# One prologue rebuilt: batch 0 ahead, distances in half blocks between projections, context products in the last pair

## The chip, the core and the metric

The kernel runs on one core of one Trainium2 chip. The time is device microseconds of a whole execution. Below it stand the five engines: TensorE (PE, with its weight loads PEld), VectorE (DVE), ScalarE (ACT), GpSimd (POOL), and the queue SP, which issues the DMAs. Each works through its own instructions in order and waits on semaphores.

## What is computed

One decoder layer over x (2, 1024, 256), in float32: a distance attention with 16 heads of width 64, a cross attention over a context of 77 rows, and a mixture of 8 experts. What the change touches is the first, and the keys and values of the second:

```python
P = X @ W_in + b_in                    # X = layernorm(x); Q, K, V, G for 16 heads
W = (EPS + sqrt(max(q2 + k2 - 2 Q K^T, 0))) ** -2
W = W / (EPS + sum(W))                 # over the keys
H = G * (W @ V)
x = x + H @ W_out + b_out
k, v = ctx @ Wk.T + bk, ctx @ Wv.T + bv        # cross attention, 77 rows for each batch
```

## The kernel before, in words

The work of the first attention is cut into 16 pairs of heads: pairs 0 to 7 are the 16 heads of batch 0, pairs 8 to 15 those of batch 1 (`PAIRS`, `QP` = 8). Each pair has T = 1024 tokens as 8 key blocks of 128 (`SB`), the two heads side by side. HALF is 512 tokens. All products are made from high and low parts (`_hi`, `_lo`), so a projection is 12 matmuls of 128x512 (`STEPS`), and a block of distances 16 (four terms, two heads, two halves).

What is done for a pair, by engine:
- TensorE: `project_qk` (Q, then K, through the bank `ps_p`), `norm_q` and `norm_k` (squared norms), `project_g`, `project_v`, `turn_v`, then for each block `distances` (L510, into `ps_s`) and, one pair later, `values` (L522) and `row_sums` (L535).
- VectorE: copies out of the banks with the bias (`copy_q` L852, `copy_k` L858, `copy_g` L891, `copy_vt` L886, `copy_v` L895), high and low parts (`split_high`, `split_low`, L864 to L870), `norm_rows` (L874, L876), `copy_k2` (L881), and for each block the two `guard` operations (L927, max with 0, one for each head) which free the banks for the next block.
- ScalarE: roots (L1364), then after a table load logarithm (L1370) and exponential (L1372) over chunks of blocks.
- GpSimd: splits weights (L1488, L1492), squares Q and K (L1505, L1511), and adds up half of the row sums.

In the pair loop, pair p's values, pair p+1's distances and pair p+2's Q and K projections are interleaved. Before it stands a prologue, and the change is in it. It runs: SP issues all of x, the constants, biases, context, cross-attention weights, and then the first projection weights. VectorE takes the statistics of all 16 row tiles, ScalarE the square root (L1341), VectorE normalises 16 tiles (L827). Meanwhile TensorE makes the context products (L410, L414), which VectorE later turns into `k_blk` and `v_x` (`context`). TensorE turns the rows of both batches (L425, 8 groups of 4), ScalarE and VectorE write their high (L1346) and low (L833) parts. Then Q, K of pair 0, the norms, Q, K of pair 1, G and V of pair 0, and after these the eight blocks of distances of pair 0, each of which waits until both guards of the block before are done (`max_ok`). There is no planner; the order on each engine is that of the written code.

Of the kernel before, what the change touches and what calls it, by code (L numbers as in the profile page):

```python
# [5 lines left out]
ALU = mybir.AluOpType  # L6
# [7 lines left out]
P = 128  # L14
# [78 lines left out]
def program(nc, x, ctx_t, mask, w_in, b_in, w_out, w_x, b_cols, rows_in, gate_w, w1, w2, w3, consts, r_consts, out):  # L93
    with ExitStack() as ctx:
# [114 lines left out]
        x_first = wts[:, 1, 0:4, :].rearrange("p a (b d) -> p (a b) d", d=D)  # L209
# [40 lines left out]
        names = ("x_in", "c_in", "stats_ok", "aggr_ok", "std_ok", "rstd_ok", "xn_ok", "tr_ok", "xnt_ok",  # L250
# [17 lines left out]
        C_IN = 16 * (1 + 8 + DC + 4 + 1 + 4 + 1 + 1)  # L268
        xn = wts[:, 0, 0:4, :].rearrange("p a (b d) -> p (a b) d", d=D)
# [4 lines left out]
        def _(sp):  # L274
            sp.dma_start(x_first, x.rearrange("b (n p) d -> p (b n) d", p=P)).then_inc(S_.x_in, 16)
            sp.dma_start(cst[:], consts).then_inc(S_.c_in, 16)
            for k in range(4):
                for h in range(2):
                    src = b_in[k // 2, (k % 2) * DH:(k % 2 + 1) * DH]
                    sp.dma_start(b_all[h * DH:(h + 1) * DH, k], src).then_inc(S_.c_in, 16)  # L280
            for c in range(DC):
                sp.dma_start(ctx_sb[:, c], ctx_t[c * P:(c + 1) * P]).then_inc(S_.c_in, 16)
            for k in range(4):
                sp.dma_start(w_x_sb[:, k], w_x[k].rearrange("(c p) n -> p c n", p=P)).then_inc(S_.c_in, 16)
            sp.dma_start(b_qk_x[:], b_cols).then_inc(S_.c_in, 16)
            for k in range(4):
                sp.dma_start(brow[:, k], rows_in[k:k + 1].partition_broadcast(P)).then_inc(S_.c_in, 16)
            sp.dma_start(mask_i[:], mask.partition_broadcast(P)).then_inc(S_.c_in, 16)
            sp.dma_start(gate_sb[:], gate_w.rearrange("(c p) e -> p c e", p=P)).then_inc(S_.c_in, 16)
# [21 lines left out]
            load_qk(0, 0)  # L311
            load_vg(0, 0)

# [3 lines left out]
            load_qk(1, 1)  # L317
            load_qk(2, 2)
# [86 lines left out]
        def _(pe):  # L405
            pe.wait_ge(S_.c_in, C_IN)
            for b in range(B):
                for c in range(DC):
                    for cc in range(DC):
                        pe.matmul(ps_o[:, (b * DC + c) * KC:(b * DC + c + 1) * KC], w_x_sb[:, 1, cc, c * P:(c + 1) * P],  # L410
                                  ctx_sb[:, cc, b * KC:(b + 1) * KC], start=cc == 0, stop=cc == DC - 1)
            for b in range(B):
                for cc in range(DC):
                    mm = pe.matmul(ps_o[0:KC, HALF + b * D:HALF + (b + 1) * D], ctx_sb[:, cc, b * KC:(b + 1) * KC],  # L414
                                   w_x_sb[:, 2, cc, :], start=cc == 0, stop=cc == DC - 1)
            mm.then_inc(S_.kv_mm, 1)
            pe.wait_ge(S_.xn_ok, 1)
            for n in range(NT // 4):
                for c in range(DC):
                    k = n * DC + c  # L420
                    if k >= 4:
                        pe.wait_ge(S_.xnt_ok, k - 3)
                    dst = ps_s[:, (k % 4) // 2, (k % 2) * 512:(k % 2) * 512 + 512]
                    for i in range(4):
                        mm = pe.transpose(dst[:, i * P:(i + 1) * P], xn[:, 4 * n + i, c * P:(c + 1) * P], ident)  # L425
                    mm.then_inc(S_.tr_ok, 1)
            pe.wait_ge(S_.xnt_ok, NT // 4 * DC)
# [11 lines left out]
            def project_qk(p, i0, i1, rows_before):  # L439
                for i in range(i0, i1):  # L440
                    if i == 0:
                        pe.wait_ge(S_.wqk_ok, 2 * p + 2)
                        if rows_before is not None:
                            pe.wait_ge(S_.rln_ok, rows_before)
# [7 lines left out]

            def norm_q(n):
# [8 lines left out]
            def norm_k(n):  # L462
                pe.wait_ge(S_.sqk_ok, n + 1)
                pe.wait_ge(S_.qn_ok, n + 1)
                for b in range(SB):
                    mm = pe.matmul(ps_s[:, 0, 2 * b:2 * b + 2], k_sq[:, b * P:(b + 1) * P], cst[:, C_SK:C_SK + 2], start=True, stop=True)
                mm.then_inc(S_.k2_mm, 1)

            def project_v(n, keys):
                pe.wait_ge(S_.wvg_ok, 2 * n + 2)  # L470
                pe.wait_ge(S_.k_cp, keys)
# [4 lines left out]
            def project_g(n):  # L476
                if not (isinstance(n, int) and n == 0):
                    pe.wait_ge(S_.max_ok, NB * n + NB)
                for i in range(STEPS):
                    mm = project_step(ps_s[:, 1], wvg_hi, wvg_lo, n, 1, i)  # L480
                mm.then_inc(S_.g_proj, 1)

            def turn_v(n):
                pe.wait_ge(S_.vt_ok, n + 1)
                pe.wait_ge(S_.kv_ok, 1)
                if not (isinstance(n, int) and n == 0):
# [5 lines left out]
            def distances(n, b):  # L492
                if b == 0:
# [4 lines left out]
                    done = 1 if isinstance(n, int) and n == 0 else n  # L498
                    pe.wait_ge(S_.vt_ok, done)
                    pe.wait_ge(S_.g_ok, done)  # L500
                else:
# [1170 lines left out]
```

## Time and profile before

| | us |
|---|---|
| median of 3 runs (lowest, highest) | 1659.29 (1654.48, 1662.12) |
| the profiled execution | 1656.51 |
| its span, first to last instruction | 1654.3 |
| mean granted TensorE clock | 0.936 |
| PE busy | 1453.9 (88%) |
| VectorE busy | 1039.0 (63%) |
| ScalarE busy | 926.9 (56%) |
| GpSimd busy | 643.0 (39%) |

The attention's pair loop ends at about 956 us of the span, the cross attention and the experts take the rest. Shares of the whole span are averages over these stages. The first slices of the profile's time line show TensorE at four to six tenths before it settles at nine.

### The profile page before, as it was taken

The page shows a single profiled execution, that of the slowest core. Times are in us where ns is not written, and L with a number is a line of the kernel's source. Part 1 is how long each engine was busy: PE and PEld are TensorE (multiplying, and loading weights), DVE is VectorE, ACT ScalarE, POOL GpSimd, SP SyncE. Part 2 cuts the span into 40 slices and gives each one's busy share as a digit, 9 for nine tenths or more (in the row PEclk, how much of TensorE's full clock was granted, in tenths as well). Part 3 has the DMA queues.
Part 4 walks back from the last instruction along what each step waited for, and adds up shares of the span by engine and source line. Part 5 has one row for each costly group of instructions (what it writes and reads, how often), then busy time and mean ns, then how long its engine had stood idle before and what let it go on. Part 6 is the DMA issues. An engine that isn't in the chain of part 4 may idle for free. (4 is left out here: it accounts for less than half of the span.)

```text
span 1654.3 us, 23058 instructions
## 1 busy us (share of the span) xinstructions
PE 1453.9 (88%) x7425; PEld 934.3 (56%) x7426; DVE 1039.0 (63%) x1352; ACT 926.9 (56%) x643; POOL 643.0 (39%) x476
## 2 busy tenths in 40 slices
PE   4659999999999999999998759988996499999996
PEld 3434555455554555555554347777775366666664
DVE  6457889889988889889888555455555521222121
ACT  1049888998889888998889812222222022222221
POOL 1304546554465546554455432212211133333331
PEclk9769999999999999999999779889886699999998
DMA  4000000000000000000000042111120033333312
GB/s 125 19 7 1 14 26 25 13 13 25 25 19 13 19 25 25 13 13 25 19 13 13 5 142 91 38 46 49 38 90 19 13 79 92 75 84 84 81 29 70
DMA packets 67467, 66.90 MB, mean 40 GB/s; under 512 B 5136, under 2 KB 59920, under 8 KB 67408
## 3 DMA queue, kind: packets, MB, share of 16 engines
q1 hardware_dynamic: 60144, 56.58, 10.5%
q0 software_dynamic: 7296, 9.97, 3.6%
q8 instruction: 16, 0.26, 0.1%
q14 instruction: 11, 0.09, 0.0%
HBM read 48.70 MB, written 19.92 MB: 41 GB/s over the span
## 5 line engine op out<-in xcount | busy, mean ns | idle before, releaser
L927 DVE TENSOR_SCALAR wts<-ps_s,k 128x1024 f32<-128x1024 f32 x256 | 316.9, 1280 | 108.4 <-PE ps_s L510 89.3
L1519 POOL TENSOR_TENSOR v_aug<-v_aug,wts 128x1024 f32<-128x1024 f32 x96 | 255.9, 2666 | 295.6 <-ACT wts L1372 291.1
L1364 ACT ACTIVATE wts<-wts 128x4096 f32<-128x4096 f32 (+1 forms) x80 | 232.0, 2936 | 140.9 <-DVE wts L927 140.7
L522 PE MATMUL ps_o<-wts,g_r 128*64 128x512 f32 x1024 | 253.8, 618 | 12.2 <-ACT wts L1372 12.0
L1370 ACT ACTIVATE wts<-wts,eps_d 128x4096 f32<-128x4096 f32 (+1 forms) x80 | 241.7, 3021 | 0.2
L1372 ACT ACTIVATE wts<-wts 128x4096 f32<-128x4096 f32 (+1 forms) x80 | 235.3, 2941 | 2.5
L736 PE MATMUL ps_s<-wts,qk 128*128 x608 | 198.0, 469 | 3.1 <-issue 2.3
L1300 DVE TENSOR_TENSOR wts<-rinv,ps_s 128x352 f32<-128x352 f32 x76 | 39.6, 521 | 253.9 <-ACT rinv L1437 170.9
L510 PE MATMUL ps_s<-q_hi,k_hi 64*128 64x512 f32 x512 | 117.2, 452 | 58.2 <-DVE wts L927 49.7
L916 DVE TENSOR_TENSOR v_aug<-v_aug,wts 128x1024 f32<-128x1024 f32 x96 | 158.7, 1653 | 10.0 <-ACT wts L1372 9.7
L736 PEld LDWEIGHTS ps_s<-wts,qk 128*128 128x128 f32 x608 | 110.5, 191 | 64.8 <-issue 17.0
L522 PEld LDWEIGHTS ps_o<-wts,g_r 128*64 128x64 f32 x1024 | 64.1, 139 | 134.5 <-issue 111.2
L1437 ACT ACTIVATE rinv<-ps_s 128x352 f32<-128x352 f32 x76 | 35.3, 465 | 179.2 <-PE ps_s L736 165.7
L510 PEld LDWEIGHTS ps_s<-q_hi,k_hi 64*128 64x128 f32 x512 | 49.8, 188 | 133.0 <-DVE wts L927 105.7
L761 PE MATMUL ps_o<-wts 128*128 x456 | 112.2, 388 | 0.7 <-DVE wts L1308 0.7
L510 PE MATMUL ps_s<-q_lo,k_hi 64*128 64x512 f32 x512 | 104.6, 402 | 0.0
L510 PE MATMUL ps_s<-q_hi,k_lo 64*128 64x512 f32 x512 | 104.5, 401 | 0.0
L510 PE MATMUL ps_s<-q_n,k_n 64*128 64x512 f32 x512 | 104.2, 399 | 0.0
L1416 ACT ACTIVATE v_aug<-v_aug 128x1232 f32<-128x1232 f32 x16 | 19.7, 1232 | 148.7 <-POOL v_aug L1567 148.7
L761 PEld LDWEIGHTS ps_o<-wts 128*128 128x128 f32 x456 | 80.5, 189 | 21.7 <-issue 13.6
L587 PE MATMUL ps_o<-wts,qk 128*128 128x256 f32 x256 | 85.8, 496 | 6.5 <-DMA qk<-h_t 6.5
L1567 POOL TENSOR_TENSOR v_aug<-v_aug,lmax 128x1232 f32<-128x1232 f32 x16 | 36.0, 2249 | 114.5 <-DVE lmax L1064 114.5
(219 smaller groups left out, 2413.2 us busy)
## 6 DMA issues: line engine op xcount, KB each, us to landing
wts<-in_w SPq DMA_DIRECT2D x16, 704.0 KB
h_t<-o_raw SPq DMA_DIRECT2D x16, 512.0 KB, 2.6
qk<-h_t SPq DMA_DIRECT2D x16, 512.0 KB, 4.1
wts<-in_w SPq DMA_DIRECT2D x8, 640.0 KB
wts<-in_x SPq DMA_DIRECT2D x2, 2048.0 KB, 8.7
raw_qk<-in_w_in SPq DMA_DIRECT2D x32, 128.0 KB, 2.2
raw_vg<-in_w_in SPq DMA_DIRECT2D x32, 128.0 KB, 2.2
acc<-wts SPq DMA_DIRECT2D x17, 128.0 KB, 1.7
```

The source lines that it names most:

```text
L510: mm = pe.matmul(ps_s[:, h, t], k[r], q[r, t], start=i == 0, stop=i == len(terms) - 1)
L522: mm = pe.matmul(ps_o[r, t], v_pair[:, b, r], wts[:, h, b, t], start=b == 0, stop=b == SB - 1)
L587: mm = pe.matmul(bank_a[:, 0:D], h_tile[:, q, :], w_o[:, q, :], start=q == 0, stop=q == H // 2 - 1)
L736: mm = pe.matmul(ps_s[:, k, j * HALF:j * HALF + DEH], y_tt[:, par, c], w12[:, bass.ds(slot, 1), k, c, j * DEH:(j + 1) * DEH], start=c == 0 ...
L761: mm = pe.matmul(ps_o[:, HALF:HALF + D], h_tt[0:m, par, n], w3_sb[0:m, bass.ds(slot, 1), n], start=n == 0, stop=n == NC - 1)
L916: dve.tensor_tensor(acc_w[:, 1], acc_w[:, 1], wts[:, 1, b], ALU.add).then_inc(S_.addb_ok, 1)
L927: dve.tensor_scalar(wts[:, h, b, :], ps_s[:, h, :], k2[:, 2 * b + h:2 * b + h + 1], 0.0, ALU.add, ALU.max).then_inc(S_.max_ok, 1)
L1300: dve.tensor_tensor(h_sb[:, par, t], s_up[:, t], ps_s[:, 1, j * HALF:j * HALF + DEH], ALU.mult).then_inc(S_.hm_ok, 1)
L1364: act.activation(chunk(start, end), chunk(start, end), ACT.Sqrt).then_inc(S_.sqrt_ok, 1)
L1370: act.activation(chunk(start, end), chunk(start, end), ACT.Ln, bias=eps_d[:, 0:1]).then_inc(S_.ln_ok, 1)
L1372: act.activation(chunk(start, end), chunk(start, end), ACT.Exp, scale=-2.0).then_inc(S_.w_ok, 1)
L1519: pool.tensor_tensor(acc_w[:, 0], acc_w[:, 0], wts[:, 0, b], ALU.add).then_inc(S_.add_ok, 1)
```

## The change

The x of batch 0 and that of batch 1 are loaded, measured and normalised apart. Batch 1's statistics are taken by VectorE between batch 0's steps and its normalisation is done by GpSimd. The high parts of pair 0 are written by ScalarE. K of pair 0 is projected into `ps_s[:, 1]`, so it doesn't wait for the copy of Q out of `ps_p`; G of pair 0 goes into `ps_p`. The distances of pair 0 are released and guarded in halves of 512 tokens (`fill_s`, `fill_ok`). Between them stand the Q and K projections of pair 1, four matmuls at a time, and the turning of batch 1's rows, in two lots. G of pair 0 is projected behind the last block. The context products and VectorE's work on them stand in the last pair. The SP queue issues in another order: first weights ahead of the biases, the context's loads behind the second Q and K weights. ScalarE's table for the square root is loaded at the start.

```diff
         @block.sync
-            sp.dma_start(x_first, x.rearrange("b (n p) d -> p (b n) d", p=P)).then_inc(S_.x_in, 16)
-            sp.dma_start(cst[:], consts).then_inc(S_.c_in, 16)
+            sp.dma_start(x_first[0], x[0].rearrange("(n p) d -> p n d", p=P)).then_inc(S_.x_in, 16)
+            sp.dma_start(cst[:], consts).then_inc(S_.cst_in, 16)
...
+            load_qk(0, 0)
             for k in range(4):
                 for h in range(2):
                     src = b_in[k // 2, (k % 2) * DH:(k % 2 + 1) * DH]
-                    sp.dma_start(b_all[h * DH:(h + 1) * DH, k], src).then_inc(S_.c_in, 16)
+                    sp.dma_start(b_all[h * DH:(h + 1) * DH, k], src).then_inc(S_.cst_in, 16)
+            sp.dma_start(x_first[1], x[1].rearrange("(n p) d -> p n d", p=P)).then_inc(S_.xb_in, 16)
+            load_vg(0, 0)
+            sp.wait_ge(S_.zero_ok, 1)
+            sp.dma_start(y_rows[NT * P:], zeros).then_inc(S_.zero_out, 16)
+            sp.dma_start(acc[NT * P:], zeros).then_inc(S_.zero_out, 16)
+            load_qk(1, 1)
             for c in range(DC):
                 sp.dma_start(ctx_sb[:, c], ctx_t[c * P:(c + 1) * P]).then_inc(S_.c_in, 16)
...
         @block.tensor
+            def turn_rows(k):
+                n, c = k // DC, k % DC
+                if n < 2:
+                    pe.wait_ge(S_.xn_ok, n + 1)
+                    dst = ps_s[:, k // 2, (k % 2) * HALF:(k % 2 + 1) * HALF]
+                else:
+                    pe.wait_ge(S_.xnb_ok, 1)
+                    pe.wait_ge(S_.v_ok, 1)
+                    if k >= 6:
+                        pe.wait_ge(S_.xnt_ok, k - 1)
+                    dst = ps_o[:, (k % 2) * HALF:(k % 2 + 1) * HALF]
+                for i in range(4):
+                    mm = pe.transpose(dst[:, i * P:(i + 1) * P], xn[n // 2][:, 4 * (n % 2) + i, c * P:(c + 1) * P], ident)
+                mm.then_inc(S_.tr_ok, 1)
...
+            def project_first():
+                pe.wait_ge(S_.wqk_ok, 2)
+                for k, out in enumerate((ps_p, ps_s[:, 1])):
+                    for i in range(STEPS):
+                        if k == 0 and i % (STEPS // 2) == 0:
+                            pe.wait_ge(S_.xnt_ok, 2 + 2 * (i // (STEPS // 2)))
+                        mm = project_step(out, wqk_hi, wqk_lo, 0, k, i)
+                    mm.then_inc((S_.q_proj, S_.k_proj)[k], 1)
...
                 for th in range(2):
+                    if fill and b:
+                        pe.wait_ge((S_.fill_ok, S_.max_ok)[th], (b, 2 * b)[th])
                     t = slice(th * HALF, (th + 1) * HALF)
...
+                    if fill:
+                        mm.then_inc(S_.fill_s, 1)
...
             def pair(p, first=False, ahead=2):
 
+                if ahead == 0:
+                    context()
...
-            project_qk(0, 0, 2 * STEPS, None)
+            pe.wait_ge(S_.cst_in, CST_IN)
+            for k in range(4):
+                turn_rows(k)
+            project_first()
             norm_q(0)
-            norm_k(0)
-            pe.wait_ge(S_.k_cp, 1)
-            project_qk(1, 0, 2 * STEPS, None)
-            project_g(0)
-            project_v(0, 2)
-            turn_v(0)
+            project_v(0, None)
+            norm_k(0, ps_o)
             for b in range(SB):
                 distances(0, b)
+                if b == 0:
+                    turn_v(0)
+                if b == 3:
+                    turn_rows(4)
+                    turn_rows(5)
+                elif b < 7:
+                    project_qk(1, 4 * (b - (b > 3)), 4 * (b - (b > 3) + 1), None)
+                if b == 4:
+                    turn_rows(6)
+                    turn_rows(7)
+            project_g(0, ps_p, 2)
             norm_q(1)
-            norm_k(1)
+            norm_k(1, ps_s[:, 0])
...
         @block.vector
+            def guard_halves(b):
+                for th in range(2):
+                    t = slice(th * HALF, (th + 1) * HALF)
+                    dve.wait_ge(S_.fill_s, 2 * b + th + 1)
+                    for h in range(2):
+                        g = dve.tensor_scalar(wts[:, h, b, t], ps_s[:, h, t], k2[:, 2 * b + h:2 * b + h + 1], 0.0, ALU.add, ALU.max)
+                        if th:
+                            g.then_inc(S_.max_ok, 1)
+                        elif h:
+                            g.then_inc(S_.fill_ok, 1)
...
-            context()
+            row_stats(1)
             copy_q(0)
+            row_aggr(1)
             copy_k(0)
-            split_high(0)
+            row_rstd(1)
             split_low(0)
             norm_rows(0)
             copy_k2(0)
-            copy_q(1)
+            copy_vt(0, 1)
+            for b in range(SB):
+                if b == 4:
+                    dve.wait_ge(S_.zero_out, 32)
+                guard_halves(b)
+                if b == 0:
+                    copy_v(0)
+                if b == 3:
+                    copy_q(1)
+                    turned_low(4)
+                    turned_low(5)
+                if b == 4:
+                    turned_low(6)
+                    turned_low(7)
             copy_k(1)
+            split_high(1)
+            norm_rows(1)
             copy_g(0)
-            copy_vt(0, 1)
-            copy_v(0)
...
-            split_high(1)
             split_low(1)
-            norm_rows(1)
             copy_k2(1)
...
         @block.scalar
+            act.preload_act_table_set("sqrt_and_others")
+            row_std(0)
+            for k in range(4):
+                turned_high(k)
+            act.wait_ge(S_.q_ok, 1)
+            act.activation(q_hi[:], q32[:], ACT.Copy)
+            row_std(1)
+            act.wait_ge(S_.k_cp, 1)
+            act.activation(k_hi[:], k32[:], ACT.Copy).then_inc(S_.hi_ok, 1)
...
                 for start, end in ROOTS:
+                    if isinstance(n, int) and start in (2, 4):
+                        turned_high(start + 2)
+                        turned_high(start + 3)
...
         @block.gpsimd
             split_qk(1)
+            pool.wait_ge(S_.rstd_ok, 2)
+            for i in range(SB):
+                bn = pool.tensor_scalar(xn[1][:, i, :], x_first[1][:, i, :], mean_var[:, SB + i, 0:1], rstd[:, SB + i:SB + i + 1],
+                                        ALU.subtract, ALU.mult)
+            bn.then_inc(S_.xnb_ok, 1)
             square_q(1, 1)
```

`row_stats(b)`, `row_aggr(b)`, `row_rstd(b)`, `row_std(b)`, `turned_low(k)` and `turned_high(k)` are the old loops, cut to one batch or to one group of rows. VectorE's `context` is unchanged but reads `ps_s[:, 0]` in place of `ps_o`, and is called behind `add_first` of the last pair.

## Rows read from the trace of the kernel before

**Rows 1.** Stretches: from:to, length, busy us and count of each engine, PEclk, DMA share, GB/s

```profile
0.00:73.30 73.30, 39.14 (x158) 29.67 (x159) 42.53 (x90) 6.04 (x10) 14.79 (x18) 0.88 0.27 78
73.30:119.40 46.10, 26.53 (x131) 17.45 (x131) 21.01 (x18) 12.77 (x4) 8.86 (x10) 0.69 0.04 12
119.40:129.40 10.00, 6.39 (x22) 4.42 (x22) 6.17 (x8) 9.85 (x6) 0.00 (x0) 0.67 0.00 0
...
237.90:925.00 687.10, 649.22 (x3544) 357.74 (x3544) 595.26 (x486) 630.35 (x247) 362.37 (x207) 1.00 0.05 18
```

**Rows 2.** Order of time, first 73 us: start, us, engine, line, what, idle before

```profile
3.44 5.04 SPq L280 DMA_DIRECT2D gl<-in_b_in  x8
...
9.17 5.33 DVE L817 BATCH_NORM_STATS2 stats<-wts 128x6 f32<-128x256 f32 x16 [7.43 <-DMA wts<-in_x]
...
14.53 1.17 DVE L821 BATCH_NORM_AGGREGATE mean_var<-stats 128x2 f32<-128x6 f32 x16
...
15.78 1.28 ACT L1341 ACT_TABLE_LOAD   x1 [15.78 <-DVE mean_var L821]
...
17.70 8.23 DVE L827 TENSOR_SCALAR wts<-wts,mean_var,rstd 128x256 f32<-128x256 f32 x16
...
38.66 1.90 POOL L1505 TENSOR_TENSOR qk_sq<-qk 128x1024 f32<-128x1024 f32 x1 [13.85 <-DVE qk L852]
...
50.93 1.28 DVE L876 SCALAR_TENSOR_TENSOR q_n<-q_n,cst,ps_s 128x1024 fp32r<-128x1024 f32 x1
...
52.35 3.55 PE L466 MATMUL ps_s<-cst,k_sq 128*128 128x2 f32 x16 [8.95 <-DVE q_n L876]
```

**Rows 3.** Order of time, TensorE, pair 1's Q and K; then PE and clock

```profile
55.76 1.20 PE L434 MATMUL ps_p<-xn_hi,wqk_hi 128*128 128x512 f32 x2
...
60.17 0.69 PE L434 MATMUL ps_p<-xn_lo,wqk_hi 128*128 128x512 f32 x2
...
62.24 0.73 PE L434 MATMUL ps_p<-xn_hi,wqk_hi 128*128 128x512 f32 x2 [1.38 <-DVE qk L852]
...
64.67 0.63 PE L434 MATMUL ps_p<-xn_lo,wqk_hi 128*128 128x512 f32 x2
...
57.00:58.00 1.00, 1.00 (x3) 0.50 0.00 0
```

**Rows 4.** Order of time, second block of distances; then a group of 128x512 operations

```profile
78.06 0.80 PE L510 MATMUL ps_s<-q_hi,k_hi 64*128 64x512 f32 x2 [2.67 <-DVE wts L927]
...
81.89 2.48 DVE L927 TENSOR_SCALAR wts<-ps_s,k 128x1024 f32<-128x1024 f32 x2 [3.88 <-PE ps_s L510]
...
L833 DVE TENSOR_TENSOR xn_lo<-ps_s,xn_hi 128x512 fp32r<-128x512 f32 x8 | 4.9, 682 | 1.4 <-ACT xn_hi L1346 1.4
```

**Rows 5.** Order of time, the second table load and three copies of k2

```profile
121.39 1.28 ACT L1367 ACT_TABLE_LOAD   x1
...
129.19 0.17 DVE L881 COPY k<-ps_s 128x16 f32<-128x16 f32 x1 [3.73 <-PE ps_s L466]
...
184.71 0.17 DVE L881 COPY k<-ps_s 128x16 f32<-128x16 f32 x1
...
237.75 0.17 DVE L881 COPY k<-ps_s 128x16 f32<-128x16 f32 x1
```

**Rows 6.** One line of GpSimd: ns shortest/median/longest, first and last start

```profile
L1488 POOL TENSOR_TENSOR wqk_hi<-raw_qk,cst x32: 607/611/1059, 19.1 to 809.9; 128x256 fp32r<-128x256 f32 x32
```

**Rows 7.** Order of time: the context products now, and the last pair

```profile
18.35 3.69 PE L410 MATMUL ps_o<-ctx_sb,w_x_sb 128*128 128x77 f32 x16 [18.35 <-DMA gate_sb<-in_gate_w]
...
21.84 3.62 PE L414 MATMUL ps_o<-w_x_sb,ctx_sb 128*77 128x256 f32 x8
...
33.80 2.93 DVE L977 TENSOR_TENSOR k_blk<-k_raw,cst 128x616 f32<-128x616 f32 x4
...
932.74 4.53 DVE L916 TENSOR_TENSOR v_aug<-v_aug,wts 128x1024 f32<-128x1024 f32 x2 [4.89 <-ACT wts L1372]
932.75 6.00 PE L522 MATMUL ps_o<-wts,g_r 128*64 128x512 f32 x16 [5.31 <-ACT wts L1372]
```

More of the change, by code:

```diff
@@ L416, in _ @@
[L416 to L426, printed above, removed]
@@ new lines, in context @@
+            def context():
+                pe.wait_ge(S_.c_in, C_IN)
+                pe.wait_ge(S_.max_ok, NB * PAIRS)
+                for b in range(B):
+                    for c in range(DC):
+                        for cc in range(DC):
+                            pe.matmul(ps_s[:, 0, (b * DC + c) * KC:(b * DC + c + 1) * KC], w_x_sb[:, 1, cc, c * P:(c + 1) * P],
+                                      ctx_sb[:, cc, b * KC:(b + 1) * KC], start=cc == 0, stop=cc == DC - 1)
+                for b in range(B):
+                    for cc in range(DC):
+                        mm = pe.matmul(ps_s[0:KC, 0, HALF + b * D:HALF + (b + 1) * D], ctx_sb[:, cc, b * KC:(b + 1) * KC],
+                                       w_x_sb[:, 2, cc, :], start=cc == 0, stop=cc == DC - 1)
+                mm.then_inc(S_.kv_mm, 1)
@@ L460, in norm_q, with norm_k @@
                 mm.then_inc(S_.norm_mm, 1)
-            def norm_k(n):
+            def norm_k(n, out):
                 pe.wait_ge(S_.sqk_ok, n + 1)
-                pe.wait_ge(S_.qn_ok, n + 1)
+                if not (isinstance(n, int) and n == 0):
+                    pe.wait_ge(S_.qn_ok, n + 1)
                 for b in range(SB):
-                    mm = pe.matmul(ps_s[:, 0, 2 * b:2 * b + 2], k_sq[:, b * P:(b + 1) * P], cst[:, C_SK:C_SK + 2], start=True, stop=True)
+                    mm = pe.matmul(out[:, 2 * b:2 * b + 2], k_sq[:, b * P:(b + 1) * P], cst[:, C_SK:C_SK + 2], start=True, stop=True)
                 mm.then_inc(S_.k2_mm, 1)
@@ L484, in turn_v @@
                 pe.wait_ge(S_.vt_ok, n + 1)
-                pe.wait_ge(S_.kv_ok, 1)
-                if not (isinstance(n, int) and n == 0):
+                if isinstance(n, int) and n == 0:
+                    pe.wait_ge(S_.k2_ok, 1)
+                else:
                     pe.wait_ge(S_.oraw_ok, n)
@@ L492, in distances @@
             def distances(n, b):
+                fill = isinstance(n, int) and n == 0
                 if b == 0:
@@ L497, in distances @@
                     pe.wait_ge(S_.k2_ok, n + 1)
[L498 to L501, printed above, removed]
+                    if not fill:
+                        pe.wait_ge(S_.vt_ok, n)
+                        pe.wait_ge(S_.g_ok, n)
+                elif not fill:
                     pe.wait_ge(S_.max_ok, NB * n + 2 * b)
@@ L838, in _ @@
+            for k in range(4):
+                turned_low(k)
+            dve.wait_ge(S_.cst_in, CST_IN)
             for h in range(2):
@@ L940, in pair @@
                 add_first(p)
+                if ahead == 0:
+                    context()
                 for b in range(SB):
```

171 lines of the change are left out of this document (88 added, 83 removed).

## The prediction, before the result was known

> **What bounds the kernel now.** I read the stretches first [rows 1], then the order of time up to the first values product, then the two ends of the pair loop. The span of 1654.3 us begins with a prologue up to 129.4 us, in which no value product runs. In the pair loop that follows TensorE is busy 649 of 687 us and ScalarE 630 of 687 at a granted clock of 1.00, and the copy of the key norms (L881), which opens each pair, returns after 53.04 us once the loop is even (184.71 to 237.75) and after 55.5 us in the first pair (129.19 to 184.71) [rows 5]. Nothing in the loop or behind it is edited, except that the cross attention's context products are put into the last pair. So the change is worth what it takes from the time at which the second pair's key norms are copied, 129.4 us, and I cut the prologue into three parts that end at events which both kernels have: the first distance matmul (73.3), the end of the last guard of pair 0 (119.4), and the copy of k2 for pair 1 (129.4).
>
> In the first part nothing overlaps: 16 row statistics wait until all of x has landed (9.17), 16 normalisations take 8.23 us, and TensorE is busy 39 of 73 us [rows 1, 2]. In the second part TensorE and VectorE alternate: a block of distances waits 2.67 us for the guards of the block before, the two guards take 2.48 us after waiting 3.88 us for TensorE [rows 4]. Eight blocks take 46.1 us, 5.8 each, with TensorE busy 26.5 of 46.1 at a mean granted clock of 0.69 [rows 1]. Twelve projection matmuls take 5.1 us (55.76 to 60.86) where the granted clock is 0.50 and 3.06 us (62.24 to 65.30) later, at twice the pace [rows 3]. From these I use 0.255 and 0.43 us for a projection matmul, and 1.85 and 3.4 us for a block of distances (16 matmuls, the two heads side by side, by the same spacing of 0.23 and 0.43 for each pair).
>
> **Part one, start to first distances: 73.3 becomes 35.** All times are from the span's start.
> - x of batch 0 is half the bytes. It lands between 4.6 (half of 9.17) and 9.17; I take 6.0, since a part of the 9.17 is issue and latency that doesn't halve [rows 2].
> - Eight statistics (5.33/2 = 2.67) and eight aggregates (0.6) end at 9.3. The square root no longer loads its table there (1.28 us, now done while x travels); root and reciprocal, 0.8 with their waits, end at 10.1. Eight normalisations are half of 8.23, 4.1, so 14.2 [rows 2].
> - The constants and biases must be in before TensorE turns rows and before GpSimd splits weights. The bias DMAs are issued until 8.5 now [rows 2] and until about 9.5 with the two weight DMAs put ahead of them; I take them landed at 11.4. Both are needed only at 12. Had they landed 2.5 us later, the sum would grow by 2.
> - Four groups are turned; VectorE's four low parts of 0.68 (0.61 apart) end at 16.8 [rows 4]. Bias and constant copies, 0.6, and the statistics of batch 1, 2.67, which stand ahead of the copy of Q, hold VectorE until 20.1. The second x DMA is issued at about 10 and may land as late as 17.4 without a cost; 4 us more would cost 2.
> - TensorE starts the Q projection at 15.5. Q and K are 24 matmuls, 6.1 us at full clock, 10.3 at half: K ends at 21.6 or 25.8, I take 24. Copy of K 1.28, to 25.3; ScalarE's high part 1.1, to 26.4; two low parts (1.3 to 1.7 each, GpSimd being at work), to 29.3; two norm-row operations 1.21 + 1.28 [rows 2], to 31.9.
> - Beside that TensorE has norm_q (1.9 or 3.6), V (3.05 or 5.1) and norm_k (2.0 or 3.55 [rows 2]) after the square of Q (GpSimd, 1.90 [rows 2]). From 24.3 this ends at 31.3 at full clock and 36.5 at half. It is the later of the two chains. With the k2 copy I take 35. All at full clock gives 30, all at half clock 39.
>
> Off this part go batch 1's statistics and normalisations, the pair 1 projections (55.8 to 65.3) and G 0, which move behind the first distances, and the context products: TensorE's 7.1 us (18.35 to 25.46) lay beside the normalisations and VectorE's beside the Q projection, so that removal alone is worth 0.5 us at most [rows 7].
>
> **Part two, first distances to last guard: 46.1 becomes 28.7.** A half block is guarded while the other half is computed. TensorE: 8 blocks of 1.85 = 14.8, 24 projection matmuls at 0.255 = 6.1, turning V 1.1, turning four row groups 2.4, together 24.4 us. VectorE: 32 guards of 128x512. No such guard is in the trace; its nearest rows are the 128x512 subtraction, 0.682 long and 0.61 apart, and the whole guard, two in 2.48, as the dear end (it would cost 1.24 too if width didn't matter) [rows 4]. I take 0.65, 20.8 in all; plus copy of V 1.2, copy of Q 1 1.28, four low parts 2.4: 25.7 us. The two engines are near even, so a step costs the longer of them. Added to that: the first half block before VectorE can start, 0.9, and a stall at blocks 4 and 5: VectorE's low parts 6 and 7 wait for ScalarE's high parts, which are queued behind a root of 3.6 us; behind the low parts wait the guards of block 5, and for these TensorE. About 2 us. Sum 28.7. At half clock TensorE's 24.4 becomes 44.6, and that is then the length of this part.
>
> GpSimd normalises batch 1 in this part, eight 128x256 operations that take the place of VectorE's. The row groups 4 to 7 wait for them, on TensorE between block 3 and block 4. GpSimd has 128x256 operations of 0.61 to 1.06 us and a 128x1024 one of 1.90 [rows 2, 6]; I take 0.7. They start at about 30 (behind the split of the second weights) and are needed at 48, so up to 2.2 us each is free; ahead of pair 1's squares they delay nothing that isn't due later. No price below 0.3 could be seen either, for the same reason.
>
> **Part three, last guard to k2 of pair 1: 9.9 becomes 13.5.** This gets longer. The last projection ends before block 7, but K 1 is copied behind the guards (1.28), and only then may G 0 take its bank: 12 matmuls 3.05 (5.1), norm_q 1.9 (3.6), norm rows 2.5, G's copy 1.28, two low parts 2.45, k2 0.2. With waits 13.1, half clock 16.9; I take 13.5. The first weights for pair 0 need the roots, which end 2 us after the last guard, then the table load: the values of block 0 are ready 7 us after the guards, earlier than k2, as now (121.39 against 129.19 [rows 5]).
>
> **The far end: 0.** The context products, 24 matmuls in 7.1 us [rows 7], are now ahead of the last pair's values. TensorE then has an idle 5.31 us before its blocks 2 and 3, VectorE 4.89 us before its sums at the same point, both waiting for ScalarE's exponentials [rows 7]. TensorE starts the products when it ends the row sums of pair 14, at 921.2, ends at 928.4, catches up blocks 0 and 1 (3.9) at 932.3 and meets block 2 at 932.75. VectorE's part (2.93 for the masks of K [rows 7], some 2 us for the rest) ends at about 933.4, 0.7 late, and the sums wait again at 942. If that cover weren't there it would be 7.1 + 4.9 = 12. Their loads, 13 DMAs, move behind the wait for the first weight split; they land by 30 and are used at 921. The weight loads behind them wait for later splits anyway. In the loop, code and counts are the same, so I leave 53.04 a pair.
>
> **Sum.** 35 + 28.7 + 13.5 = 77.2 in place of 129.4: 52.2 us less. The profiled execution took 1656.5 with its 1654.3 span, so 1604.3; the median of the runs is 2.8 higher than the profiled one: 1607.
>
> **Clock, the skill's rule.** TensorE: Matmul & The Clock Gate ("What's actually happening") of the Trainium skill says that idleness throttles the array and sustained activity releases it. The trace agrees: 0.69 granted in the alternating part, 1.00 in the busy loop [rows 1]. By the rule part two runs at 2.4 GHz; by the 0.69 of the old rows it would take some 8 us more than my 28.7.
>
> **Rivals.**
> 1. The clock stays low, at 1.2 GHz through the whole new prologue: 39 + 44.6 + 16.6 = 100, 29 us less, 1630. For: part one still has waits, as the old one had (0.50 at 57 us [rows 3]). Against: part two has TensorE work nearly always ready. A clock that is low in part one and in half of part two gives about 1618. Together 0.20.
> 2. All at full clock: 30 + 27.7 + 12.5 = 70, 59 less, 1600; if the first pair also loses its 2.5 us of excess over 53.04, 1597.5. 0.13.
> 3. The change doesn't do what it says: a half guard costs nearly a whole one, 32 x 1.24 + 4.9 = 45 plus stalls, 48 for part two. Then 35 + 48 + 13.5 = 96.5, 33 less, 1626. Against it is the 0.61 spacing of 128x512 operations [rows 4]. 0.03.
> 4. Slower than before: GpSimd's eight normalisations, a form that it has nowhere in this trace. From the turning of row group 4 to the k2 copy there are 27.5 us; the time of k2 is 30 + 8n + 27.5 once n is over 2.2 us, and reaches 129.4 at n = 9.0. At 10 us each: 1667. Row groups wait, TensorE waits, the clock falls. Its rows, 0.61 to 1.90 whole, speak against it [rows 2, 6]. 0.02 with slower; another 0.02 lies within 0.5% (n from 8 to 10).
>
> **Numbers.** The forecast has 0.60, its own range is 1601 to 1614. 0.5% is 8 us, about what a measurement of this kernel tells from no change. Range 1597 to 1626: it leaves out the whole half-clock case and the sides of no change. Faster by over 0.5%: 0.95, within 0.02, slower 0.03 (rival 4 and 0.01 for a loop that no longer falls into 53.04).
>
> **What would show it.** The first distance matmul at 30 to 39; the last guard 27 to 32 us later with half guards 0.6 to 0.7 apart; granted clock near 1.00 between; the k2 copy of pair 1 at 70 to 84 and behind it the old gaps of 53.04; GpSimd's eight operations under 2.2 us each; in the last pair the gaps before blocks 2 and 3 gone and the rest not shifted. Wrong would be: a loop period that is not 53.0, a clock near 0.5 in part two, or an x of batch 1 that lands after 20.

## The result, and the profile after

| | before | changed |
|---|---|---|
| median, us (lowest, highest) | 1660.07 (1654.48, 1662.12), 4 runs | 1604.31 (1601.77, 1606.96), 4 runs |
| the profiled execution, its span | 1656.51, 1654.3 | 1606.14, 1604.3 |
| mean granted clock | 0.936 | 0.945 |

The ratio is 0.9668, 95% interval 0.9645 to 0.9691: 51 to 59 us less. Forecast was 1607, range 1597 to 1626. Measured twice more, beside the experiments below, the same kernel gave 0.9653 (0.9636 to 0.967) and 0.9681 (0.9661 to 0.9702). One of the six executions in experiment 5 was in a slow state (2158.32 us at a granted clock of 0.636) and is left out of its median.

The three parts of the prologue, in the stretches that answer to [rows 1] (columns as there):

```profile
0.00:31.30 31.30, 16.25 (x72) 13.04 (x73) 22.95 (x63) 6.28 (x9) 14.35 (x19) 1.00 0.56 166
31.30:62.20 30.90, 28.17 (x176) 19.16 (x176) 27.46 (x40) 14.73 (x8) 10.87 (x9) 0.95 0.07 18
62.20:74.40 12.20, 8.17 (x36) 5.73 (x38) 10.74 (x10) 12.01 (x7) 7.91 (x9) 0.91 0.15 43
```

TensorE is now busy 28.2 of 30.9 us beside the guards, VectorE 27.5, and the granted clock is 0.95 in place of 0.69. The part behind the guards got longer, from 9.9 to 12.1. Now the order of time for the events that part them (the first distances, VectorE's copies of k2 for pairs 1, 2 and 3), which answer to [rows 5]:

```profile
31.36 0.79 PE L537 MATMUL ps_s<-q_hi,k_hi 64*128 64x512 f32 x2 [0.66 <-DVE k L938]
...
74.23 0.17 DVE L938 COPY k<-ps_s 128x16 f32<-128x16 f32 x1
...
129.90 0.17 DVE L938 COPY k<-ps_s 128x16 f32<-128x16 f32 x1
...
182.94 0.17 DVE L938 COPY k<-ps_s 128x16 f32<-128x16 f32 x1
```

| | forecast | changed | before |
|---|---|---|---|
| first distances start | 35 | 31.4 | 73.3 |
| to the last guard's end | 28.7 | 30.9 | 46.1 |
| to the end of the k2 copy, pair 1 | 13.5 | 12.1 | 9.9 |
| sum | 77.2 | 74.4 | 129.4 |

The first pair takes 55.7 us (55.5 before) and the next 53.04, as before. At the k2 copy of pair 1 the changed kernel is 55.0 us ahead, at the last pair's row sums 55.8 (900.79 against 956.60), yet the two spans differ by 50.0. The 5.6 us between are in the stretch from the first output product of the attention to the end. That stretch, columns as in [rows 1], in the kernel before, in this profile, and in two later profiles of the changed kernel:

```profile
965.02:1654.30 689.28, 608.56 (x2953) 463.30 (x2953) 254.24 (x667) 145.21 (x330) 176.38 (x201) 0.90 0.23 61
```

```profile
909.43:1604.30 694.87, 614.13 (x2953) 467.00 (x2953) 254.38 (x667) 144.87 (x330) 174.78 (x201) 0.89 0.23 61
```

```profile
907.84:1598.80 690.96, 610.73 (x2953) 464.71 (x2953) 254.34 (x667) 144.98 (x330) 174.80 (x201) 0.90 0.23 61
```

```profile
908.38:1603.00 694.62, 613.43 (x2953) 466.86 (x2953) 254.31 (x667) 145.04 (x330) 175.04 (x201) 0.89 0.23 61
```

The same 2953 matmuls are busy for 608.6, 614.1, 610.7 and 613.4 us. Nothing there was given back by the change: all twelve profiles told of here have this stretch between 689.3 and 695.4, with no regard to the kernel.

The last pair, which now has the context products (order of time; TensorE, then VectorE), answers to [rows 7]:

```profile
866.33 1.89 PE L431 MATMUL ps_s<-w_x_sb,ctx_sb 128*77 128x256 f32 x8
868.16 3.65 PE L552 MATMUL ps_o<-wts,g_r 128*64 128x512 f32 x16
876.95 5.67 PE L552 MATMUL ps_o<-wts,g_r 128*64 128x512 f32 x16 [5.14 <-ACT wts L1466]
```

```profile
873.04 2.93 DVE L1016 TENSOR_TENSOR k_blk<-k_raw,cst 128x616 f32<-128x616 f32 x4
875.89 0.74 DVE L1019 TENSOR_TENSOR v_x<-ps_s,brow 77x256 f32<-77x256 f32 x2
876.93 4.53 DVE L973 TENSOR_TENSOR v_aug<-v_aug,wts 128x1024 f32<-128x1024 f32 x2 [0.29 <-ACT wts L1466]
886.27 4.55 DVE L973 TENSOR_TENSOR v_aug<-v_aug,wts 128x1024 f32<-128x1024 f32 x2 [4.81 <-ACT wts L1466]
```

VectorE's wait of 4.89 us ahead of its sums is down to 0.29, so its work on the context just fits, and the next wait is 4.81 as in the kernel before. The prediction expected TensorE's gap ahead of block 2 to vanish too. It did not: TensorE still waits 5.14 us there (5.31 before). The products take half of what they took at the start (8 matmuls in 1.89 us against 3.62 [rows 7]), all 24 some 3.7 us (864.49 to 868.16) and not the 7.1 that the prediction laid into that gap, and they mostly take the place of TensorE's waits ahead of blocks 0 and 1 (0.58 and 1.81 us in the kernel before, none now).

### The profile page after: what moved, and what is told of

The parts are those of the page before. It is cut to its first block and busy times, and to the rows that moved or that the text cites. A ratio compares the mean times of both kernels' runs of the same rounds, so it can differ in the third digit from the quotient of the medians.

```text
span 1604.3 us, 23093 instructions
## 1 busy us (share of the span) xinstructions
PE 1440.8 (90%) x7425; PEld 926.5 (58%) x7426; DVE 1032.5 (64%) x1359; ACT 928.5 (58%) x646; POOL 650.2 (41%) x484
## 5 line engine op out<-in xcount | busy, mean ns | idle before, releaser
L984 DVE TENSOR_SCALAR wts<-ps_s,k 128x1024 f32<-128x1024 f32 x240 | 297.1, 1279 | 86.3 <-PE ps_s L537 66.0
L629 PE MATMUL ps_o<-wts,qk 128*128 128x256 f32 x256 | 90.8, 520 | 6.7 <-DMA qk<-h_t 6.7
L1605 POOL TENSOR_TENSOR k_sq<-norms 128x1024 f32<-128x1024 f32 x16 | 42.1, 2631 | 110.9 <-DVE norms L915 110.9
```

What stands on the lines that cost most here:

```text
L629: mm = pe.matmul(bank_a[:, 0:D], h_tile[:, q, :], w_o[:, q, :], start=q == 0, stop=q == H // 2 - 1)
L984: dve.tensor_scalar(wts[:, h, b, :], ps_s[:, h, :], k2[:, 2 * b + h:2 * b + h + 1], 0.0, ALU.add, ALU.max).then_inc(S_.max_ok, 1)
```

## Experiments

Each is read by three landmarks: start of the first distances, end of the last guard, copy of k2 for pair 1. For the changed kernel they are 31.1 to 31.5, 60.6 to 62.3 and 72.6 to 75.6 over three profiles. The third scatters by 3 us in one and the same kernel, so a difference of that size at the k2 copy alone tells nothing; the last guard is the steadier landmark.

**1. Whole blocks, projections between (e1_whole).**

```diff
                 for th in range(2):
-                    if fill and b:
-                        pe.wait_ge((S_.fill_ok, S_.max_ok)[th], (b, 2 * b)[th])
+                    if fill and b and th == 0:
+                        pe.wait_ge(S_.max_ok, 2 * b)
...
-                    dve.wait_ge(S_.fill_s, 2 * b + th + 1)
+                dve.wait_ge(S_.fill_s, 2 * b + 2)
```

and VectorE's two guards of a block are 128x1024 again.

> The changed kernel with the distances of pair 0 released and guarded in whole blocks again; the projections of pair 1 stay between them. Theory A (halves let VectorE guard one half while TensorE computes the other): a block then costs distances 1.85 + guards 2.48 + two handovers 0.2 = 4.5 us, times 8, plus about 2 us of row-group work: the part from first distances to last guard goes from 30.9 to about 38, the k2 copy of pair 1 from 74.2 to about 81, the time from 1604 to about 1611. Rival B (VectorE is the bound of this part either way, so halves are worth nothing): 30.9 stays within 1 us, time 1604. Rival C (the halves carried nearly all of the gain of this part): it goes back to 46, time 1619.

Measured: 31.4, 68.9, 82.4; 1613.5 us, ratio 0.9733 (0.9686 to 0.9779). The part takes 37.5 us. One period in the order of time, TensorE and VectorE:

```profile
38.71 0.64 PE L440 MATMUL ps_p<-xn_hi,wqk_hi 128*128 128x512 f32 x2
40.79 0.50 PE L537 MATMUL ps_s<-q_hi,k_hi 64*128 64x512 f32 x2 [1.45 <-DVE wts L990]
```

```profile
38.26 2.48 DVE L990 TENSOR_SCALAR wts<-ps_s,k 128x1024 f32<-128x1024 f32 x2 [1.09 <-PE ps_s L537]
42.95 1.28 DVE L990 TENSOR_SCALAR wts<-ps_s,k 128x1024 f32<-128x1024 f32 x1 [2.21 <-PE ps_s L537]
```

Each engine waits for the other again, 4.69 us from guard to guard (38.26 to 42.95). Theory A holds: halves are worth 7 to 8 us. The interleaved projections still keep the clock at 1.00.

**2. Projections ahead, halves kept (e2_ahead).**

```diff
             norm_k(0, ps_o)
+            project_qk(1, 0, 2 * STEPS, None)
             for b in range(SB):
...
-                elif b < 7:
-                    project_qk(1, 4 * (b - (b > 3)), 4 * (b - (b > 3) + 1), None)
```

and VectorE's copy of Q 1 stands ahead of the guards.

> The changed kernel with pair 1's Q and K projections in one piece ahead of the first distances (and the copy of Q 1 there), halves kept. Theory A (the projections are TensorE time of 6 us that fits beside VectorE's guards): first distances at about 40 instead of 31.4 (two projections and the copy between them, 8.7 us), the part of the distances shorter by 1 to 3 us since VectorE alone bounds it, k2 copy of pair 1 at about 80, time about 1610. Rival B (they were never beside anything, TensorE is the bound of the distances): part two shrinks by the same 6 us and more, k2 copy at 74 to 76, time 1604 to 1606. Rival C (TensorE now idles between half blocks and its granted clock falls): part two grows to 36 or more, k2 copy at 87 or later, 1617.

Measured: 42.5, 69.2, 81.2; 1612.7 us, ratio 0.9727 (0.968 to 0.9773). The first distances come 11.1 us later, the stretch of distances is 26.75 us at clock 1.00 with VectorE busy 25.1 of it. So rival B is out: VectorE nearly alone bounds that stretch then, and the projections do fit beside it, at a price of 3 to 4 us there. Theory A's 40 was missed by 2.5 since Q's twelve matmuls ran at half pace (order of time, TensorE):

```profile
32.63 1.19 PE L440 MATMUL ps_p<-xn_hi,wqk_hi 128*128 128x512 f32 x2 [1.92 <-DVE qk_sq L942]
...
37.03 1.06 PE L440 MATMUL ps_p<-xn_lo,wqk_hi 128*128 128x512 f32 x2
39.46 0.74 PE L440 MATMUL ps_p<-xn_hi,wqk_hi 128*128 128x512 f32 x2 [1.38 <-DVE qk L908]
```

**3. Both (e3_both):** the two edits together.

> Both edits: whole blocks, projections ahead. What is left of the change is batch 0 first and the context products at the end. Theory A with the clock as a part of it: TensorE is busy 1.85 of 4.5 us in part two, the granted clock falls to about 0.7 as in the kernel before, and part two takes about 46 again: k2 copy at 74.2 + 15 + 9 = 98, time about 1628, which is more than the two single edits together (7 + 6 = 13). Rival B (clock has no share, the two edits add up): k2 copy at 87 to 88, time 1617.

Measured: 42.4, 83.4, 97.5; 1628.6 us, ratio 0.9825 (0.9775 to 0.9874). The two stretches behind the first distances, columns as in [rows 1]:

```profile
42.42:83.40 40.98, 23.84 (x153) 16.60 (x152) 23.33 (x22) 14.83 (x8) 1.89 (x1) 0.86 0.00 0
83.40:97.53 14.13, 10.16 (x36) 6.93 (x38) 10.52 (x9) 14.00 (x7) 7.90 (x9) 0.74 0.13 37
```

The time is as theory A had it, the place less so: 41.0 us at 0.86, not 46 at 0.7. The two edits alone cost about 8 and 7 us at the k2 copy, together 22 to 25, so they don't add up. With only one of the two edits the clock stays at 1.00 in this stretch, with both it is 0.86. But the clock is only a part of the surplus. Measured from the 60.6 of the second profile of the changed kernel, the last guard comes 8.3 and 8.6 us later with one edit and 22.8 with both, 5.9 more than the sum. About 3.5 of that is the slower clock (41.0 us here against the 37.5 of experiment 1, with the same whole blocks). About 2.7 is something else: with halves the stretch gets shorter when the projections leave it (29.5 to 26.75, experiment 2), while in whole blocks they lay in TensorE's waits, where taking them out gives nothing back: a period at full clock is 4.68 us here and 4.69 in experiment 1. The 0.74 behind the last guard says nothing on this, since the unchanged kernel had it too in one profile (61.0 to 75.7). Why the clock is 0.86 here and 0.69 in the kernel before, with the same alternation, stays open. What remains of the change here, batch 0 first and the context products last, is worth 31 us by the medians (1659.85 to 1628.63).

**4. More work for GpSimd (e4_pool3).**

```diff
             pool.wait_ge(S_.rstd_ok, 2)
...
+            for i, dst in enumerate(spare):
+                pool.tensor_scalar(dst, x_first[1][:, i % SB, :], mean_var[:, SB + i % SB, 0:1], rstd[:, SB + i % SB:SB + i % SB + 1],
+                                   ALU.subtract, ALU.mult)
             for i in range(SB):
```

> The changed kernel with 16 more of GpSimd's 128x256 operations ahead of the eight that normalise batch 1 (their results go to unused buffers), 19.4 us more on GpSimd at the 1.21 us each that the trace shows. Theory A (GpSimd's work is free up to the turning of row group 4, which stands at 45.2 while GpSimd is done at 40.3, and costs one for one beyond): row group 4 is turned at 59.7, k2 copy of pair 1 at 74.2 + 14.5 = 88.7, time about 1618.5. Rival B (GpSimd's operations also hold VectorE at the port that they share, so VectorE's guards get longer than 0.68 us each): guards above 0.8 us and a loss above 18 us. Rival C (what the row groups wait for is not on the path): under 3 us lost.

Measured: 31.5, 77.3, 92.0; 1619.9 us, ratio 0.977 (0.9722 to 0.9818). TensorE around the turning of row group 4 in the order of time, then the stretch that follows, TensorE's busy time first and the granted clock third from the right, then VectorE's half guards while GpSimd works (group, busy, mean ns of one):

```profile
59.71 1.97 PE L418 MATMUL ps_o<-cst,wts 128*128 128x128 f32 x8 [15.72 <-POOL wts L1647]
61.61 0.79 PE L537 MATMUL ps_s<-q_hi,k_hi 64*128 64x512 f32 x2
```

```profile
60.00:64.00 4.00, 4.00 (x20) 3.18 (x20) 1.58 (x3) 2.88 (x3) 1.52 (x1) 0.50 0.00 0
```

```profile
L992 DVE TENSOR_SCALAR wts<-ps_s,k 128x512 f32<-128x512 f32 x16 | 10.9, 744 | 1.3 <-PE ps_s L537 1.3
```

Row group 4 is turned at 59.7, as expected. Rival B falls: the guards take 744 ns, the same as in the changed kernel. But the loss at the k2 copy is 16.4 to 19.3, not 14.5. Its parts: TensorE is at row group 4 at 44.0 and waits 15.7 us there; the two later profiles of the changed kernel turn it at 43.6 and 44.0, only the first at 45.2, which made the expected delay too small. After the wait TensorE's granted clock is 0.50 until 64, but from the turning to the last guard this run takes 17.6 us where the three profiles take 17.0, so that costs 0.6. From 76 to 84 the clock is low again (0.60), and the part behind the guards takes 14.7 us at 0.74; one profile of the unchanged kernel has 14.6 at 0.74, so this share can't be put down to GpSimd. GpSimd's slack is real, and exceeding it costs the delay one for one and little more. The guards read one operand from a PSUM bank; an operation of VectorE with two inputs, neither in PSUM, did take longer beside GpSimd (the low parts of Q in the changed kernel: 2.02 us at 25.1 beside it, 1.22 at 72.0).

**5. The clock alone (e5_busy),** in the kernel before:

```diff
             for b in range(SB):
                 distances(0, b)
+                for i in range(8 if b < 7 else 0):
+                    th = i % 2
+                    pe.matmul(ps_p[:, th * HALF:(th + 1) * HALF], k_hi[:, b * P:(b + 1) * P], q_hi[:, th * HALF:(th + 1) * HALF],
+                              start=True, stop=True)
```

> The kernel before, with 8 matmuls of 128x512 that compute nothing needed put behind each of the first seven blocks of distances of pair 0, where TensorE waits for the guards. They only keep TensorE busy (8 x 0.23 = 1.9 us in a wait of 2.6). Theory A (part of the gain is the clock): the granted clock in the stretch goes from 0.69 to above 0.9, a block from 5.8 to about 4.6 us, the stretch from 46.1 to about 37, time 9 us less, about 1651. Rival B (the wait alternation alone sets it, the clock has no share): no change, 1660. Rival C (work in the gap only delays the next block): slower by 1 us a block, 1667.

Measured: 76.1, 113.6, 123.4; 1653.1 us (five runs), ratio 0.9954 (0.9939 to 0.9969). The stretch of the distances, columns as in [rows 1], and VectorE's guards of blocks 0 and 1 in it:

```profile
76.15:113.65 37.50, 32.23 (x188) 21.97 (x188) 21.03 (x18) 12.79 (x4) 8.89 (x10) 1.00 0.05 14
```

```profile
78.41 2.48 DVE L931 TENSOR_SCALAR wts<-ps_s,k 128x1024 f32<-128x1024 f32 x2 [0.92 <-PE ps_s L510]
83.09 2.48 DVE L931 TENSOR_SCALAR wts<-ps_s,k 128x1024 f32<-128x1024 f32 x2 [2.21 <-PE ps_s L510]
```

56 matmuls that nobody needs, some 13 us of added TensorE work (56 at 0.23), make the stretch 8.6 us shorter: clock 1.00 for 0.69, 4.7 us a block for 5.8. So of the 15 us that the distances gained in the change, about 8.6 can be had by the clock alone and 7 to 8 are the halves. The whole run gained 6 us by the medians (1659.36 before) and 8 by the ratio. In this profile the first part was 2.9 us longer than in that of before, and the stretch behind the attention 6.1 us longer (695.4), so its span shows none of the gain; the k2 copy comes 5.8 us earlier. Experiment 1, with whole blocks and a full clock, has the same 37.5 us.

**6. Context products last, alone (e6_ctxlast),** in the kernel before: TensorE's 24 matmuls and VectorE's `context` called in the last pair as in the change. The 13 loads stay where they were.

> The kernel before with one part of the change alone: context products and VectorE's work on them moved into the last pair. Theory A: TensorE's 7.1 us lay beside the normalisations, VectorE's 4.8 beside the Q projection; worth 0.5 us at most, time 1660 to 1659. Rival B: the 4.8 us of VectorE were on the path: 5 us less, 1655. Rival C: they now cost in the last pair: 5 us or more slower.

Measured: 73.3, 118.5, 128.3; 1658.8 us, ratio 0.999 (0.9979 to 1.0002). No difference that can be told, as theory A has it; a loss of 5 us is excluded, and so is a gain of 5. This is the sum of what the move brings in front and costs in the last pair.

**7. Context products in front, in the changed kernel (e7_ctxfront):** `context()` ahead of the first row groups, the 13 loads ahead of batch 1's x.

> The changed kernel with the context products back at the front and their 13 loads ahead of batch 1's x. Theory A (with batch 0 alone the rows are ready at 12.9, long before the context has landed at about 18.5, so what was worth 0.5 us in the kernel before is now worth the whole wait and the products): first distances 11 to 14 us later, at 43 to 45, time about 1616. Rival B (as in the kernel before, they lie beside VectorE's work): 0 to 2 us, 1604 to 1606.

Measured: 48.1, 77.5, 89.5; 1620.5 us, ratio 0.9763 (0.9743 to 0.9783). TensorE in the order of time, then VectorE:

```profile
17.67 3.69 PE L426 MATMUL ps_o<-ctx_sb,w_x_sb 128*128 128x77 f32 x16 [17.67 <-DMA gate_sb<-in_gate_w]
21.16 3.62 PE L430 MATMUL ps_o<-w_x_sb,ctx_sb 128*77 128x256 f32 x8
24.57 2.49 PE L418 MATMUL ps_s<-cst,wts 128*128 128x128 f32 x16
```

```profile
33.17 0.74 DVE L1018 TENSOR_TENSOR v_x<-ps_o,brow 77x256 f32<-77x256 f32 x2
33.84 2.69 DVE L861 BATCH_NORM_STATS2 stats<-wts 128x6 f32<-128x256 f32 x8
36.45 1.26 DVE L908 TENSOR_SCALAR qk<-ps_p,b_pair 128x1024 f32<-128x1024 f32 x1
```

The move that is worth nothing in the old prologue is worth 16.7 us at the first distances of the new one. Expected were 11 to 14. Missed was VectorE: its part on the context stands, with batch 1's statistics, ahead of the copy of Q (36.45; 20.95 in the changed kernel), so it is on the path too. The loads move here as well, which they don't in experiment 6: what shows of that is TensorE's wait for the last of them until 17.67. The later x of batch 1 costs nothing, VectorE's statistics of it (33.84) follow its other work without a wait.

**8. The changed kernel again (after_again).**

> The changed kernel unchanged. In the two profiles the k2 copy of pair 1 comes 55.0 us earlier, but the span is only 50.0 us shorter: 5.6 us are missing behind the last pair. Theory A (they are scatter of the granted clock in the later stages, and the runs of one kernel spread over 5 to 8 us): the medians differ by 54 to 57, and a second profile has a later part that is not tied to the first one's. Rival B (something behind the pair loop is slower in the changed kernel): every profile has that part 5 us longer than the 689.3 of before, and the medians differ by 50.

Measured: 31.1, 60.6, 72.6; 1602.3 us, ratio 0.9653. The stretch behind the attention is 691.0 here, 694.9 in the first profile: theory A.

**9. A further version (b1_part3), with the changed kernel beside it (after_5).**

```diff
+                if b == 7:
+                    copy_k(1)
                 guard_halves(b)
...
-            copy_k(1)
-            split_high(1)
-            norm_rows(1)
             copy_g(0)
+            norm_rows(1)
             split_low(1)
...
             roots(0)
+            act.wait_ge(S_.k_cp, 2)
+            act.wait_ge(S_.fill_s, 2 * SB)
+            act.activation(q_hi[:], q32[:], ACT.Copy)
+            act.activation(k_hi[:], k32[:], ACT.Copy).then_inc(S_.hi_ok, 1)
```

> A further version, aimed at the part that got longer (last guard to k2 copy of pair 1, 12.0 us): K of pair 1 is copied ahead of the guards of block 7 in place of behind them, so G can be projected as soon as the distances end; ScalarE writes the high parts of pair 1 behind its roots; VectorE's order is G, norm rows, low parts. Theory A (this part is a chain of K's copy, G, norm_q, norm rows, low parts, of which 1.3 us of copy and 3.5 us of high parts leave VectorE): k2 copy 3 to 3.5 us earlier, at about 69.2 against 72.6 in the last profile; ScalarE's weights come 2 us later, so that the values of pair 0 start at 70.6 and the first guard of pair 1 about 3 us earlier: time 1599 to 1600 against 1602 to 1603 for the changed kernel, a difference near what a measurement can tell. Rival B (ScalarE's weights, now 2 us later, bind the start of pair 0): k2 earlier, but the first guard of pair 1 not, no gain.

> The changed kernel unchanged, on the same chip as the version before it in this list, for the comparison: 1602 to 1605, k2 copy of pair 1 at 72.5 to 74.5.

Measured: 31.3, 61.0, 69.0 and 1600.6 us (1597.95 to 1603.77), ratio 0.9659 (0.9638 to 0.9681); the changed kernel beside it 31.5, 61.0, 75.6 and 1605.0 (1604.74 to 1605.78), 0.9681. VectorE in the further version:

```profile
69.03 0.17 DVE L938 COPY k<-ps_s 128x16 f32<-128x16 f32 x1 [0.56 <-PE ps_s L484]
74.06 2.36 DVE L965 TENSOR_TENSOR v_aug<-wts 128x1024 f32<-128x1024 f32 x2 [4.86 <-ACT wts L1466]
76.45 2.48 DVE L984 TENSOR_SCALAR wts<-ps_s,k 128x1024 f32<-128x1024 f32 x2
```

The k2 copy is 3.6 to 6.5 us earlier, but VectorE then waits 4.86 us for ScalarE's weights, which is what rival B named. Even so the first guard of pair 1 is 2.1 to 3.7 us earlier than in the three profiles of the changed kernel, and the last pair's sums 1.9 to 3.5 us (897.28). All five runs lie below the five beside them (medians 4.3 us apart), but the intervals of the ratios overlap. I take it as about 2 to 4 us faster, and the fastest of the versions here. It changes three things at once, so it doesn't tell what each is worth.

## Why the prediction was right, step by step

**The sum.** 52.2 us were forecast; the k2 copy of pair 1 came 55.0 us earlier and the medians differ by 55.8. The three terms were off by -3.6, +2.2 and -1.4. That they cancel in part is luck, and so is a part of the total: the k2 copy of one kernel scatters by 3 us and the stretch behind the attention by 4. Some of the working doesn't add up as written, with no effect on the forecast beyond 0.1 us: the terms of part two give 28.6 and not 28.7, part three at half clock is given as 16.9 and again as 16.6, and rival 4 has 27.5 us from row group 4 to the k2 copy where the forecast's own times give 29.2 (77.2 less 48); measured were 29.0 (45.2 to 74.2).

**Part one** was 31.4 against 35. Chosen was the middle between full and half clock; from about 17.6 on the array ran at full pace. x of batch 0 landed at 6.5 for 6.0. The constants and biases had landed by 9.5, not 11.4; the issue of the x and constant DMAs took 1.1 us in place of 2.6, which is most of the difference. The normalisations took 3.49, not 4.1. The two chains ended within 0.5 us of one another, V and norm_k at 30.7 and the norm rows at 31.1; the forecast had TensorE's as the later by some 3 us. The low parts beside GpSimd took 2.02 and 1.63, where 1.3 to 1.7 was assumed for each.

**Part two** was 30.9 against 28.7 (29.5 in two later profiles, whose clock there was 1.00). Of the 2.2 us too many, 1.2 lie ahead of the first guard: it starts 2.1 us behind the first distances, not 0.9, since in this profile the granted clock is 0.50 from about 31 to 34; in the two others it starts after 1.2 us. The rest is the term that was mis-sized, the half guard. VectorE's first guards, then its groups in that stretch:

```profile
33.47 2.90 DVE L992 TENSOR_SCALAR wts<-ps_s,k 128x512 f32<-128x512 f32 x4 [1.07 <-PE ps_s L537]
```

```profile
L992 DVE TENSOR_SCALAR wts<-ps_s,k 128x512 f32<-128x512 f32 x32 | 21.9, 744 | 3.4 <-PE ps_s L537 3.4
L879 DVE TENSOR_TENSOR xn_lo<-ps_o,xn_hi 128x512 fp32r<-128x512 f32 x4 | 2.6, 678 | 0.0
```

744 ns, about 0.68 apart, for the 0.65 taken; 32 of them are 21.9 us, 1.1 more. The stall at blocks 4 and 5 that was priced at 2 us did not show: ScalarE's high parts 6 and 7 were done at 51.8 and VectorE got to its low parts at 52.1, straight from the guards of block 4. VectorE's idle time is all ahead of half guards, 3.4 us, of which 1.07 ahead of the first. So the 2 us priced for the stall are there, as short waits ahead of other guards: the size was right for a reason that was not. VectorE's copy of the projected V out of its bank (1.27 us at 31.1) is in no term; it costs next to nothing, since it lies in the wait for the first half block.

**Part three** grew as forecast, to 12.1 (13.5), and to 12.0 and 14.6 in the two later profiles. The cause that the forecast gave, K copied behind the guards, shows in the wait of G's first matmuls (TensorE; the changed kernel, then its third profile):

```profile
63.51 0.73 PE L440 MATMUL ps_p<-xn_hi,wvg_hi 128*128 128x512 f32 x2 [3.11 <-DVE norms L915]
62.24 1.22 PE L440 MATMUL ps_p<-xn_hi,wvg_hi 128*128 128x512 f32 x2 [3.10 <-DVE norms L915]
```

Behind the same wait G runs at full pace in the one and at half pace in the other (granted clock 0.74 over the part), and the part is 2.5 us longer. So 13.5 lies between two outcomes of one kernel. Experiment 9, in which K is copied earlier and two other things change, fits the cause but doesn't isolate it.

**GpSimd's normalisations,** a form nowhere in the trace of before, were taken at 0.7 us with 2.2 free. By this line of GpSimd (ns shortest, median, longest) they cost more:

```profile
L1642 POOL TENSOR_SCALAR wts<-wts,mean_var,rstd x8: 1208/1210/1231, 30.6 to 39.1; 128x256 f32<-128x256 f32 x8
```

1.21 us each is dearer than the nearest row [rows 6], and more of the margin was used: done at 40.3, needed at 45.2, which allows 1.8 each, not 2.2. Experiment 4 shows that the mechanism of rival 4 exists and is far away.

**The clock.** Rival 1 did not come: 0.95 to 1.00 in part two. Experiments 3 and 5 show the clock's share from both sides: 0.86 when halves and interleaved projections are both taken away, 1.00 when needless matmuls are put in. The Trainium skill (TensorE: Matmul & The Clock Gate, "What's actually happening") says that activity releases the throttle, and for part two these numbers agree.

**The far end** cost nothing, as forecast (55.0 us ahead at the k2 copy, 55.8 at the last pair's row sums; experiment 6). The way there was not as forecast: the 7.1 us for TensorE came from a row at half pace, and 3.7 were needed. The sentence that the removal at the front was worth 0.5 us at most holds only for the old prologue (experiment 7). It doesn't enter the sum, since part one was worked out without the context products; as a statement on that part of the change it would mislead.

**The loop** kept 53.04 us, and the first pair its excess (2.5 us before, 2.6 now).

## What to carry to other kernels

Cut a prologue at events that both versions have, and work each piece out as the later of two engines' chains. Where two engines hand a buffer back and forth, halves and filler work were both worth doing here, and either of them alone brought the clock back to 1.00 (experiments 1 and 2); the second is then worth less than it would be alone (at the k2 copy 15 to 16 us for the first of the two, 7 to 8 for the second). What a part of a rebuild is worth depends on what else was rebuilt: the context products were worth 0 in the old order and 16.7 us in the new.

## What was not expected of the hardware

- The first matmuls run at half pace while the profile shows a granted clock of 1.00. In the changed kernel (TensorE in the order of time, then a stretch):

```profile
12.87 3.65 PE L418 MATMUL ps_s<-cst,wts 128*128 128x128 f32 x16 [12.87 <-DVE wts L887]
16.31 1.19 PE L440 MATMUL ps_p<-xn_hi,wqk_hi 128*128 128x512 f32 x2
```

```profile
12.00:16.00 4.00, 3.13 (x15) 3.16 (x16) 3.23 (x8) 1.50 (x3) 1.07 (x3) 1.00 1.09 332
```

16 transposes take 3.65 us, 0.23 each; 8 of them at 45.2, at a granted clock of 1.00, take 1.09, 0.14 each. In the kernel before the context products come first and take the half pace (18.35 to 25.46, again with 1.00 in the profile), and the 32 transposes behind them take 4.58. The pace tells the clock (1.2 GHz there), the record doesn't until its first change, at about 31 and 33 us.
- A GpSimd tensor_scalar of 128x256 with two column operands takes 1.21 us, twice its 128x256 product of two tensors (0.61).
- The stretch behind the attention took 691.0, 694.6 and 694.9 us in three executions of the changed kernel, with 610.7 to 614.1 us of TensorE busy in it. That scatter of 3.9 us, 0.24% of the whole, is as large as what a step in the prologue may bring (experiment 9).
